# Landmark attention: pooling weights in a step of their own, between the pooling scores and their transposes

## The reference

```
out_local = softmax(q . k inside each block of 64, causal) . v
pa  = softmax(pool_q . kb * scale)                   # over the 64 tokens of a block
lmf = pa . vb                                        # 32 landmarks of 512
lq, lk, lv = lmf @ w_lm_qkv + b
lmf = lmf + (masked_softmax(lq . lk) . lv) @ w_lm_out + b
l2q = lmf @ w_l2t_q + b
ra  = softmax(l2q . kb * scale)
ro  = ra . vb
lmf = lmf + ro @ w_l2t_out + b
gk, gv = lmf @ w_lm_kv + b
out_global = masked_softmax(q . gk) . gv
out = ((1 - gate) * out_local + gate * out_global) @ w_out + b
```

## Time and profile before

| | |
|---|---|
| three runs | 3434.3, 3428.66, 3431.82 us; median 3431.82 |
| the profiled execution | 3433.37 us, span 3431.6 us |
| PE busy | 2818.2 us, 82% of the span |
| DVE, ACT, POOL busy | 2075.5, 1401.5, 1179.4 us |
| landmark stage | from about 1829 to 2537 us of the span |
| chain that ended last | PE 41%, DVE 10%, issue 5%, ACT 4% of the span |

### The profile page before, as it was taken

One profiled execution on the slowest core, in us unless ns is written; L12 is line 12 of the kernel. 1 busy time (PEld: TensorE's weight loads), 2 busy tenths in 40 slices (PEclk: granted clock), 3 DMA queues, 4 the chain that ended last, 5 costly groups with the idle time before them and its releaser, 6 DMA issues.

```text
span 3431.6 us, 51800 instructions
## 1 busy us (share of the span) xinstructions
PE 2818.2 (82%) x20614; PEld 1417.2 (41%) x20662; DVE 2075.5 (60%) x3282; ACT 1401.5 (41%) x2513; POOL 1179.4 (34%) x1118
## 2 busy tenths in 40 slices
PE   5888888866777675699998989889877989899877
PEld 3665655542323232244444444444532333333243
DVE  3323242332898989887755565655655757566577
ACT  3333323322555454211114454453523646465555
POOL 0443333331766665400005342525234424242000
PEclk8888898988888888899999998889787999999999
DMA  2212121221231232211034232323427435353301
GB/s 84 69 41 67 44 69 45 61 53 57 91 99 44 86 102 71 105 73 43 30 99 138 97 107 87 97 87 95 145 58 124 95 77 110 70 108 65 114 25 38
DMA packets 209377, 271.73 MB, mean 79 GB/s; under 512 B 84640, under 2 KB 117825, under 8 KB 208241
## 3 DMA queue, kind: packets, MB, share of 16 engines
q1 hardware_dynamic: 209136, 268.42, 27.9%
HBM read 187.89 MB, written 54.92 MB: 71 GB/s over the span
## 4 chain that ended last, share of the span: by engine, by line
PE 41%; DVE 10%; issue 5%; ACT 4%; POOL 2%; DMA 1%; SPq 0%; ACTq 0%; DVEq 0%; POOLq 0%
PE ps L229 8%; PE ps L1846 5%; PE ps L1857 5%; PE ps L3363 4%; PE ps L3350 3%; PE ps L3336 3%; PE ps L3295 2%; PE ps L3327 2%; PE ps L2507 1%; DVE arena L2770 1%; DVE arena L2768 1%; PE ps L2515 1%; ACT arena L3441 1%; PE ps L2565 1%; DVE arena L1427 1%
## 5 line engine op out<-in xcount | busy, mean ns | idle before, releaser
L229 PE MATMUL ps<-arena 128*128 128x512 f32 (+3 forms) x1280 | 480.4, 528 | 18.5 <-ACT arena L2607 6.1
L3540 DVE TENSOR_REDUCE arena<-ps 128x1 f32<-128x512 f32 x512 | 330.0, 686 | 221.8 <-PE ps L3336 220.6
L3441 ACT ACTIVATE arena<-ps 128x512 f32<-128x512 f32 x512 | 287.8, 597 | 276.2 <-PE ps L3350 272.7
L1459 POOL TENSOR_TENSOR arena<-arena 128x1024 f32<-128x1024 f32 x128 | 310.9, 2429 | 193.0 <-DVE arena L1451 193.0
L1475 PE MATMUL ps<-arena 128*128 128x512 f32 x512 | 267.2, 662 | 55.6 <-POOL arena L1459 55.4
L1451 DVE TENSOR_TENSOR_SCAN arena<-ps,arena 128x1024 f32<-128x1024 f32 x128 | 291.7, 2279 | 33.0 <-ACT ps L1442 33.0
L229 PEld LDWEIGHTS ps<-arena 128*128 128x128 f32 (+2 forms) x1296 | 195.5, 156 | 257.8 <-issue 180.1
L569 POOL TENSOR_TENSOR arena<-arena 128x31 f32<-128x31 f32 (+15 forms) x217 | 130.1, 600 | 333.0 <-DMA arena<-d_a 316.6
L1442 ACT ACTIVATE ps<-arena 128x511 f32<-128x511 f32 x256 | 165.1, 679 | 188.2 <-DVE arena L1451 188.0
L3350 PE MATMUL ps<-arena 99*128 99x512 bf16 x512 | 198.0, 390 | 43.6 <-ACT arena L3441 33.4
L3336 PE MATMUL ps<-arena 96*128 96x512 bf16 x512 | 201.3, 395 | 19.2 <-issue 15.7
(11 more groups left out here) (349 smaller groups left out, 5410.1 us busy)
## 6 DMA issues: line engine op xcount, KB each, us to landing
arena<-d_bc SPq DMA_DIRECT2D x32, 1024.0 KB, 5.6
arena<-d_x SPq DMA_DIRECT2D x28, 1024.0 KB, 7.0
arena<-d_parts SPq DMA_DIRECT2D x192, 128.0 KB, 4.6
d_x<-arena SPq DMA_DIRECT2D x80, 256.0 KB, 2.5
arena<-arena SPq DMA_DIRECT2D x128, 128.0 KB, 2.1
arena<-in_D_wlm SPq DMA_DIRECT2D x12, 1024.0 KB, 5.4
d_parts<-arena SPq DMA_DIRECT2D x32, 384.0 KB, 2.4
arena<-arena SPq DMA_DIRECT2D x16, 512.0 KB, 8.4
```

What stands on the lines that cost most here:

```text
L229: ins = pe.e.matmul(ps[:m, :n], lhsT(k), rhs(k), start=(k == 0), stop=(k == chunks - 1))
L1459: pool.e.tensor_tensor(h, h, s.bc[:, turn % s.SLOTS, 1], ALU.mult).then_inc(*pool.up("scan_hC"))
L3441: act.e.activation(s.E[:, k % 2, j], s.rexp.bank((u, i)), ACT.Exp).then_inc(*s.rexp.empty(act, (u, i)))
L3540: dve.e.tensor_reduce(s.mx[:, u % 2, t, h:h + 1], s.rmax.bank((u, m)), AX.X, ALU.max, negate=True).then_inc(*s.rmax.empty(dve, (u, m)))
```

## The change

CHAIN gets two members, pool_w and read_w, in which only DVE works: dve_pool_weights, which stood in the step of pool_T and read_T, has a step to itself. The chain now begins on step -2 instead of -1. So pool_s moves one step forward, pool_w stands on -1, where pool_s was, and pool_T to read_s keep their steps; read_w takes step 12, and read_T, read_v, rout, gk and gv stand one step later, on 13 to 17.

```
-    CHAIN = ["pool_s", "pool_T", "pool_v", "lq", "lk", "lv", "ls", "lpT", "lo", "loT", "lout", "l2q",
-             "read_s", "read_T", "read_v", "rout", "gk", "gv"]
+    CHAIN = ["pool_s", "pool_w", "pool_T", "pool_v", "lq", "lk", "lv", "ls", "lpT", "lo", "loT", "lout", "l2q",
+             "read_s", "read_w", "read_T", "read_v", "rout", "gk", "gv"]
...
-                yield "local", b, k, s.CHAIN[k + 1] if 0 <= k + 1 < len(s.CHAIN) else None, first + fronts(s.LOCAL_FRONT, k, b + 1)
+                yield "local", b, k, s.CHAIN[k + 2] if k + 2 < len(s.CHAIN) else None, first + fronts(s.LOCAL_FRONT, k, b + 1)
...
-        elif chain:
+        elif chain and chain not in ("pool_w", "read_w"):
             yield (chain, b), "act" if chain in ("pool_T", "read_T", "lpT", "loT") else "dve"
...
-            if chain:
+            if chain and chain not in ("pool_w", "read_w"):
                 s.pe_landmarks(pe, chain, b)
...
-            if chain in ("pool_T", "read_T"):
+            if chain in ("pool_w", "read_w"):
                 s.dve_pool_weights(dve, chain, b)
-            if chain:
+            elif chain:
                 s.dve_landmarks(dve, chain, b)
```

## The result

The kernel with the change takes 3401.09 us (median of five runs, 3387.34 to 3405.46), the kernel before 3428.66 beside it (3423.86 to 3434.3). The ratio is 0.9909, 95% interval 0.9891 to 0.9927. It is faster, and by more than forecast: 27.6 us in place of 19. Applied to the 3431.82 of before, the ratio gives 3400.6, just under the low end of the range, 3401. One execution of fill_before (4716 us) and one of fill_values (3623 us) ran in a slow state at a lower mean clock and are left out of their ratios.

A forecast was written before the change was run, and what follows sets the result against it. The prediction took the landmark stage as bound by PE, with gaps and part at the lower clock. Pooling 14.4 plus reading 4.8 made 19.2 us off 3433.37; with the runs' median 1.55 lower, it said 3413 us, range 3401 to 3426.

The forecast's parts named there:

- Pooling, 14.4 us forecast: Start of each batch: earlier weights remove PE's wait at pool_T; 3.4 + 5.9 + 5.1 + 0 us gained.
- the allowance for semaphores: Pooling, batch 1: 0.2 us left off the 3.6 us wait removed, so 3.4 us was taken.
- the forecast's 0 for batch 0: Pooling, batch 0: no gain, since PE's transposes wait for POOL's scaling, and POOL for a swapped key.
- Reading, 4.8 us forecast: End of each batch: r0 fills the wait at read_T; 1.2 us gained in each of four batches.
- I give r1 the 6.3 us that r0 had: Reading: r1, now next behind read_v, runs at the lower clock there and takes 6.3 us.
- by the three others: Reading, batch 3, without projections: 1.2 us taken as in the other batches, between bounds of 0 and 3.24.
- Clock stays up behind read_v: Rival at the reading: r1 takes 3.6 us, three batches gain 2.6 us more each; 3405 us, chance 0.17.
- the short r1 that I had named as a sign against me: Sign at the reading: a short r1 instead of about 6.2 us would show the forecast wrong, the kernel then faster.
- The tail eats the reading's gain: Rival at each batch's end: DVE near the global part decides; reading 0, pooling 10.2 us; 3422 us, chance 0.22.
- the 1 us that I named as a sign against me: Sign at the reading's end: gs0 waiting for L2818 by more than 1 us would show the forecast wrong.
- The wait only moves: Rival: PE stands as long at the next scaling or transposes; nothing gained, 3432 us, chance 0.10.
- Slower, by the clock: Rival between read_v and gs0: ten groups fall to the lower clock, 2.6 us each; 3445 us, chance 0.06.

The follow-up runs named there:

- fill_before: The kernel before with three thrown-away matmuls ahead of each wait for weights at pool_T and read_T; 3420.98 us, ratio 0.9969 to the kernel before.
- fill_values: The kernel after with two wide overwritten matmuls between the halves of read_v in each batch; 3402.3 us, ratio 0.9909 to the kernel before.
- read_only: The kernel before with only the reading half of the change, pooling left as it was; 3424.19 us, ratio 0.9992 to the kernel before.

## Why the prediction was right and where it was wrong

**The sign and, in the main, the mechanism** were right: L2431 waits no more, y3 is at full clock, batch 0 gives back at POOL what it gains, r0 is full and r1 slow behind read_v in batches 1 and 2, and DVE's chain behind gk is late next. From the end of values on step 12 of batch 1 to the start of r1 it took 14.2 us (2092.0 to 2106.24), for a forecast of 14.6 (its own terms add up to 14.4), and to the first shift of gs0 38.1, for 37.7 to 40. From read_T's start to that shift it was 33.7, a little under the 34 to 35.5 forecast. The stage gained 8.5 us more than the 19.2: 4.2 at the reading, 1.5 at the pooling, 2.9 in the small products and the global part.

**Pooling, 14.4 us forecast, 15.6 to 15.9 measured.** Batch 1 gained 3.6 to 3.8 for 3.4, batch 2 6.7 for 5.9, batch 3 5.5 for 5.1, and batch 0 between 0.1 gained and 0.5 lost for nothing. The rows were added up rightly; the allowance for semaphores wasn't needed, and some of the small groups around y3 came back to full clock as well (in batch 2 the transposes of pool_T took 0.60 us for 1.11). The group behind pool_T in batch 0, r7, had been slow too, 5.30 us before and 3.60 after:

```profile
1846.33 5.30 PE L229 MATMUL ps<-arena 128*128 128x512 f32 x8
```

That gain went into the wait for POOL as well, so the forecast's 0 for batch 0 stood.

**Reading, 4.8 us forecast, 7.2 to 13.4 measured. This is the term that failed.** "I give r1 the 6.3 us that r0 had" was applied to every batch. In batch 0 r1 took 3.70 each time, and the batch gained 4.7 to 5.3 us, not 1.2, though the four L2818 took 4.68 to 5.26 us there, beyond the 3.86 of the range's far end. In batches 1 and 2 the bounds nearly held: 2.0 to 2.2 us in batch 1 against an upper bound of 2.5, and 2.5, 2.8 and -0.2 in batch 2, the last with r0 slow too. I had put 1.2 in the middle; the four L2818 took 2.5 to 3.3 us there, so the upper end of the gain was right. In batch 3, priced at 1.2 "by the three others", the gain was -0.5, 3.3 and 0.6. The next scores waited 2.36 us for keys from ACT in all three executions, so that isn't the difference; what stood behind is. Timeline of PE, batch 3, in the first and in the second:

```profile
2428.86 0.41 PE L2506 MATMUL ps<-arena 128*64 128x512 bf16 x2 [2.36 <-ACT arena L2649]
2429.10 1.77 PE L2507 MATMUL ps<-arena 128*64 128x512 f32 x4
...
2446.89 5.01 PE L229 MATMUL ps<-arena 128*128 128x512 f32 x8
```

```profile
2425.31 0.41 PE L2506 MATMUL ps<-arena 128*64 128x512 bf16 x2 [2.36 <-ACT arena L2649]
2425.55 1.03 PE L2507 MATMUL ps<-arena 128*64 128x512 f32 x4
...
2440.94 3.60 PE L229 MATMUL ps<-arena 128*128 128x512 f32 x8
```

The last row of each is gv. The small products between ran mostly at the lower clock in the first as well, and PE waited 1.58 us there for DVE (L2795) and 1.03 for instructions.

**The clock was priced in one place only**, 2.5 and 1.7 us at y3, 4.2 in all. By fill_before it is worth about 11 us of the stage. What was left out is the small work behind each wait at read_T (2.2 us in batch 1). The forecast also gave nothing to the rest of a batch, the products between lq and read_s and the global part, which gained 2.8 to 4.1 us together in the three executions; that this is the clock too is not shown.

**Waits are not simply taken away.** PE lost 29.9 us of waiting for weights, but its idle time fell by 6.3: POOL's scaling is waited for more (35.3 us at L2515 for 21.1), ACT's exp and keys by 4.8, L2818 by 2.4. That the total still fell by 27.7 is the sum of 21.5 us less busy and 6.3 us less idle. These two don't split the cause, as fill_before shows: there about as much less busy time (21.6 us) gave only 11.2, because 10.4 us of idle time came in its place, if the filler is counted as idle. Only 1.0 of it is at the weights (8.5 us of waiting and 22.3 of filler, for 29.9). The rest is waiting for POOL's scaling (3.9 more), for DVE at L2384 and L2391 (1.9) and at one L229 (1.8), and for instructions in the value products (1.9): with PE faster, what comes next is late.

**The rivals.** "Clock stays up behind read_v" held in batch 0, the short r1 that I had named as a sign against me, and not in batches 1 and 2. Its 3405 was nearer to the result than the forecast's 3413, but by luck: it took the clock of r1 in three batches for what came from one batch and from gains that no case had. "The tail eats the reading's gain": the wait at gs0 came (2.11 us in batch 0), over the 1 us that I named as a sign against me, but it ate only part. "The wait only moves" was right of batch 0 and of the 1.52 and 0.66 at the reading. "Slower, by the clock" didn't come: the stage before had seven L229 groups of eight at the lower clock, the kernel after three (r1 twice, gv once).

**The starting point.** The three runs of before that I went by gave 3431.82; beside the later kernels it measured 3428.66, 3428.65, 3429.24 and 3429.2. These 3 us are a quarter of the miss in microseconds and none of it in the ratio.

**What stays open.** Why r1 is at full clock in batch 0 of the kernel after and not in the others, behind the same 256 products and with breaks of 1.45 to 1.52 us against 1.33 to 2.06; why r0 is full in eight of nine cases there and slow in all three of read_only, behind the same two short waits; and why the part ahead of the stage varies by 15 us.

## What to carry to other kernels

When a row shows a wait in front of PE, read the durations of everything behind it against the same instructions elsewhere, not just the next large group: the wait costs its own length and can bring the lower clock behind it, and here the second was worth 11 of 27 to 32 us by itself. A few products that are thrown away, issued into the wait, price the clock with the waits left in place; here they were worth 0.3% as they stood. Work for a waiting engine should be queued ahead of work that nobody waits for, and a step that gives it an earlier place must bring the early data with it: the new place with late weights was slower than before.

## What the runs showed of the hardware

- The granted clock can fall behind a wait of PE, but need not: behind the waits at pool_T in the kernel before, 2.49, 3.59, 3.59 and 3.60 us, the group of eight L229 took 5.30, 3.60, 6.05 and 5.30 us, where 3.60 is the time at the higher level of 2.4 GHz. Behind the four waits at read_T, 3.24 to 4.45 us, the transposes took 1.11 to 1.12 us for 0.66.
- It also falls with no wait for another engine right ahead: the eight matmuls behind the 256 narrow products of read_v took 5.4 to 6.5 us in 6 of 9 cases of the kernel after, with breaks of 1.3 to 2.1 us in the supply of instructions inside. Whether the products or the break bring it isn't told apart. In the kernel after such breaks of over 1 us came in six of the eight steps of this kind, the longest 2.96 us, behind the same number of products in each of the three executions.
- Four L2818 (two inputs and one output in SBUF) took 1.43 us beside an idle POOL and 2.50 to 5.26 beside its rotations, in the kernel before and three executions of the kernel after. The Trainium skill ("SBUF — State Buffer", SBUF: two separate sides) says that a VectorE instruction with two SBUF inputs and a GpSimd one that reads SBUF take a shared pair of ports in turn, each for its whole length. The durations agree with it: in the stretch of 5.12 us POOL ran rotations of 1.26 to 1.44 us one behind the other.
